# One root product for both pairs of K in an octonion feed-forward kernel, and three reorderings beside it

## What is computed

```
y   = einsum('bct,bcd->bdt', x, W[condition])         # one 64x64 matrix for each of 32 samples
Wq  = scale * clip(round(W / scale), -1, 1)           # scale = mean |W|: ternary weights
M   = einsum('jik,jod->koid', S_OCT, Wq)              # S_OCT: signs of the octonion product
gate, up = einsum('...id,koid->...ko', y, M_gate), ... M_up     # 8 blocks of 128 -> 8 blocks of 342 (341 used)
h   = silu(gate) * up
out = x + einsum('...id,koid->...ko', h, M_down)
```

## Time and profile before

| | |
|---|---|
| median of 3 runs | 679.83 us (679.83 to 680.08) |
| the profiled execution's own time | 679.09 us |
| its span, first to last instruction | 677.3 us |
| PE busy | 643.8 us (95%), 7010 matmuls |
| DVE busy | 516.5 us (76%) |
| POOL busy | 385.1 us (57%) |
| ACT busy | 323.2 us (48%) |
| mean granted TensorE clock | 0.986 |

### The profile page before, as it was taken

One profiled execution on the slowest core, in us unless ns is written; L12 is line 12 of the kernel. 1 busy time (PEld: TensorE's weight loads), 2 busy tenths in 40 slices (PEclk: granted clock), 3 DMA queues, 4 the chain that ended last, 5 costly groups with the idle time before them and its releaser, 6 DMA issues. The chain is left out here.

```text
span 677.3 us, 17118 instructions
## 1 busy us (share of the span) xinstructions
PE 643.8 (95%) x7010; PEld 595.5 (88%) x7010; DVE 516.5 (76%) x873; ACT 323.2 (48%) x542; POOL 385.1 (57%) x453
## 2 busy tenths in 40 slices
PE   3599899999999999999999999999999999999997
PEld 3378699899999999998998999999999999988986
DVE  1899977868776787868877698767878687787785
ACT  4847455345534545254454446254462545434440
POOL 1256685547637576348646476376754486465553
PEclk9799899999999999999999999999999999999997
DMA  9200030140003200041001300031000300021001
GB/s 345 67 2 1 1 116 15 39 155 1 2 2 102 90 2 2 1 137 55 2 2 61 132 1 2 1 126 68 1 2 6 121 1 2 2 72 55 2 1 63
DMA packets 10576, 31.50 MB, mean 47 GB/s; under 512 B 3330, under 2 KB 3330, under 8 KB 10370
## 3 DMA queue, kind: packets, MB, share of 16 engines
q1 hardware_dynamic: 9906, 28.81, 12.3%
q10 hardware_dynamic: 592, 1.61, 0.7%
HBM read 22.02 MB, written 8.39 MB: 45 GB/s over the span
## 5 line engine op out<-in xcount | busy, mean ns | idle before, releaser
L1240 PE MATMUL ps<-y_op,gate_table 128*128 128x256 f16 x1408 | 182.6, 275 | 8.2 <-DVE y_op L979 4.2
L1240 PE MATMUL ps<-y_op,up_table 128*128 128x256 f16 x1408 | 180.3, 273 | 0.2 <-ACT up_table L724 0.2
L1240 PEld LDWEIGHTS ps<-y_op,gate_table 128*128 128x128 f16 x1408 | 138.3, 99 | 27.3 <-issue 4.4
L1240 PEld LDWEIGHTS ps<-y_op,up_table 128*128 128x128 f16 x1408 | 137.9, 98 | 16.8 <-DVE up_table L895 0.7
L617 POOL TENSOR_TENSOR h_pairs<-h_f 128x256 f32<-128x256 f32 (+2 forms) x128 | 118.0, 949 | 60.0 <-ACT h_f L767 57.7
L524 POOL TENSOR_TENSOR o_sb<-o_sb,wd_sb 128x256 f32<-128x256 f32 (+1 forms) x150 | 87.4, 617 | 90.8 <-DVE wd_sb L1108 89.6
L617 POOL TENSOR_TENSOR z_f<-h_pairs 128x512 f32<-128x512 f32 (+1 forms) x80 | 103.7, 1317 | 43.0 <-DVE z_op L995 41.2
L1248 PE MATMUL ps<-third_table,y_op 128*128 128x170 f16 x1408 | 108.2, 237 | 0.6 <-ACT third_table L724 0.6
L1248 PEld LDWEIGHTS ps<-third_table,y_op 128*128 128x128 f16 x1408 | 105.1, 97 | 1.1 <-issue 0.8
L822 ACT ACTIVATE ps<-ps,small 128x512 f32<-128x512 f32 x64 | 42.4, 662 | 111.0 <-DVE ps L1009 85.0
L1401 PE MATMUL ps<-down_u,z_op 128*128 128x256 f16 (+1 forms) x768 | 92.8, 277 | 2.0 <-DVE z_op L995 2.0
(11 more groups left out here) (98 smaller groups left out, 643.2 us busy)
## 6 DMA issues: line engine op xcount, KB each, us to landing
x_in<-in_x_dram SPq DMA_DIRECT2D x8, 1024.0 KB, 5.1
o_sb<-in_x_dram SPq DMA_DIRECT2D x16, 512.0 KB, 3.7
out_dram<-o_sb SPq DMA_DIRECT2D x15, 512.0 KB, 2.7
h_op<-in_L_ffn_w_gate_dram ACTq DMA_DIRECT2D x3, 512.0 KB, 6.8
h_op<-in_L_ffn_w_up_dram SPq DMA_DIRECT2D x3, 512.0 KB, 7.4
z_op<-in_L_ffn_w_down_dram SPq DMA_DIRECT2D x1, 1536.0 KB, 11.4
out_dram<-o_sb SPq DMA_DIRECT2D x2, 256.0 KB, 2.2
cond_bd<-in_L_cond_weights_dram SPq DMA_DIRECT2D x30, 16.0 KB, 3.0
```

What stands on the lines that cost most here:

```text
L1240: mm = pe.matmul(dst, table[m][:, slot, q, :], y_op[:, op, e, :], start=(i == 0 and e == 0), stop=(i == len(terms) - 1 and e == 1))
```

## The change

- **Root product.** Both `shared_pair` products of a window hold the product of weight block `root` (slot 18) once plainly and once negated. The change makes the root product once (`root_pair`, with a new operand 14 of `y_op`, the sum of operands 12 and 13). ACT copies it to `root_sb`. The first pair's own single term is added onto it in the bank. For the second pair ACT writes the negated copy back into the bank (`seed_second_pair`) and PE adds that pair's own term. The root of the next window is made in chunk 3 of the window before it.
- **y and tables.** POOL makes operand 14. The third piece of `y` becomes 7 operands wide (it was 6). Two table slots are now sums that DVE builds, and ACT copies one slot fewer. The power-of-two scale of y is halved.
- **Third window's ternary forms.** POOL makes them, in three passes for gate and three for up, in place of two passes for each on DVE.
- **Boundary.** `y_lo` of the first two pieces stands ahead of the last two `z_lo`. POOL's last round of z begins with the half whose chunks are copied first. PE's first chunk of a tile waits for all of y and starts with the root.
- **Beginning.** The first weight sum on PE comes after one round of y (it was two). DVE sums up's second and third window (it was the third alone). `copy_slots(1, 0)` stands ahead of the sum over the down weights, and `h_scales(0)` stands after `y_lo`.

The core of the diff:

```diff
-    TOP_Y = float(2 ** 14)
+    TOP_Y = float(2 ** 13)
...
-    TERN_AFTER = {1: (1, 1), 4: (0, 2), 6: (1, 2)}
-    TABLE_AFTER = {0: (0, 1), 2: (1, 1), 5: (0, 2), 6: (1, 2)}
+    TERN_AFTER = {1: (1, 1)}
+    TABLE_AFTER = {0: (0, 1), 2: (1, 1), 4: (0, 2), 6: (1, 2)}
     DOWN_AFTER = {0: 0, 3: 1, 5: 2}
...
+    Y_PIECES = [slice(0, 4), slice(4, 8), slice(8, 15)]
...
+    root = wq[0, 0]
+    (jx, one), (jy, other) = root[0], wq[0, 1][0]
+    assert one == other == 1 and wq[1, 0] == wq[0, 1] and wq[1, 1] == weight((jx, -1))
+    ROOT_OP = 14
+    q_own = [(weight((jy, 1), (jx, -1)), 13), (weight((jy, 1), (jx, 1)), 12)]
...
-    NBUILD, NCOPY = 4, 4
+    NBUILD, NCOPY = 6, 3
...
+                pool.wait_ge(y_summed, 6 * T + 5)
+                signed_add(y_f[:, ROOT_OP], y_f[:, 12], y_f[:, 13], 1).then_inc(y_summed, 1)
...
+            def ternary_of_third(m):
+                raw_at, dst = [ap[m][THIRD][:, :, 0:LAST] for ap in (raw, tern)]
+                above = pairs_of_down[:, 0:2].rearrange("p n j o -> p (n j) o")[:, :, 0:LAST]
+                pool.wait_ge(scale_ready, 3 * (m + 1))
+                if m > 0:
+                    pool.wait_ge(third_tern_ready, m)
+                pool.tensor_scalar(above, raw_at, half[m], None, ALU.is_gt).then_inc(third_compared, 1)
+                pool.tensor_scalar(dst, raw_at, minus_half[m], None, ALU.is_lt).then_inc(third_compared, 1)
+                pool.wait_ge(third_compared, 2 * m + 2)
+                pool.tensor_tensor(dst, above, dst, ALU.subtract).then_inc(third_tern_ready, 1)
...
+                if k == NR - 2:
+                    pool.wait_ge(h_copied, NC * T + NC - 2)
                     pool.wait_ge(z_ready, n)
-                pair_up(signed_add, k, h_pairs).then_inc(pairs_ready, 1)
+                    pair_up(signed_add, k, h_pairs, (0,))
+                    pool.wait_ge(h_copied, NC * T + NC)
+                    pair_up(signed_add, k, h_pairs, (1,)).then_inc(pairs_ready, 1)
...
+                    pool.wait_ge(slots_built[1], NBUILD)
+                    ternary_of_third(0)
+                    ternary_of_third(1)
...
+            def copy_root(T, w):
+                act.wait_ge(root_done, root_of(T, w))
+                if w == THIRD:
+                    act.activation(root3_sb, bank_q3, ACT.Copy).then_inc(root_copied, 1)
+                else:
+                    act.activation(root_sb[:], bank_q, ACT.Copy).then_inc(root_copied, 1)
+            def seed_second_pair(T, w):
+                act.wait_ge(root_copied, root_of(T, w))
+                act.wait_ge(q_copied, NU * T + 2 * w + 1)
+                if w == THIRD:
+                    act.activation(bank_q3, root3_sb, ACT.Copy, scale=-1.0).then_inc(q_seeded, 1)
+                else:
+                    act.activation(bank_q, root_sb[:], ACT.Copy, scale=-1.0).then_inc(q_seeded, 1)
...
+                if c == 0:
+                    copy_root(T, 0)
...
+                if c == C3:
+                    seed_second_pair(T, THIRD)
+                if T > 0 and c % 4 == 3 and c < C3:
+                    copy_root(T, c // 4 + 1)
...
+                if c % 4 == 0 and c < C3:
+                    seed_second_pair(T, c // 4)
                 if T == 0:
+                    if c % 4 == 3 and c < C3:
+                        copy_root(T, c // 4 + 1)
...
-            for w in range(NQ - 1):
-                sum_abs_of(1, w)
+            sum_abs_of(1, 0)
             y_hi(0)
+            copy_slots(1, 0)
             act.wait_ge(down_loaded, 16)
-            sum_abs(2 * NQ - 1, raw_down_at, NQ * raw_n, abs_sum[2])
-            copy_slots(1, 0)
+            sum_abs(NQ + 1, raw_down_at, NQ * raw_n, abs_sum[2])
...
+                signed_add(slots_at(m, w, 19, 1), t[:, 7:8], t[:, 4:5], 1).then_inc(built, 1)
+                signed_add(slots_at(m, w, 20, 1), t[:, 7:8], t[:, 4:5], -1).then_inc(built, 1)
...
+            for w in range(1, NQ):
+                dve.wait_ge(up_loaded[w], 16)
+                dve.tensor_reduce(abs_sum[1][:, w:w + 1], raw[1][w].rearrange("p j o -> p (j o)"), AX.X, ALU.add,
+                                  apply_absolute_value=True).then_inc(abs_summed_dve, 1)
             y_scales(0)
-            dve.wait_ge(up_loaded[NQ - 1], 16)
-            dve.tensor_reduce(abs_sum[1][:, NQ - 1:NQ], raw[1][NQ - 1].rearrange("p j o -> p (j o)"), AX.X, ALU.add,
-                              apply_absolute_value=True).then_inc(abs_summed_dve, 1)
             scales(1)
             scales_of_ffn()
-            h_scales(0)
             y_lo(0, range(2))
             ternary_of(1, 0)
             build_table(1, 0)
             y_lo(0, range(2, NY))
+            h_scales(0)
...
+                if T + 1 < NT:
+                    y_lo(T + 1, range(2))
                 for i, k in enumerate(last_rounds(T)):
                     z_lo(T, k, NR - 2 + i)
                 if T + 1 < NT:
-                    y_lo(T + 1)
+                    y_lo(T + 1, range(2, NY))
...
+            def root_pair(T, w):
+                if w == 0:
+                    if T > 0:
+                        pe.wait_ge(q_copied, NU * T)
+                        pe.wait_ge(ud_ready, SUB * (T - 1) + 1)
+                else:
+                    pe.wait_ge(q_copied, NU * T + 2 * w)
+                if w == THIRD:
+                    if T == 0:
+                        for m in range(2):
+                            pe.wait_ge(slots_built[m], NBUILD * NQ)
+                            pe.wait_ge(slots_copied[m], NCOPY * NQ)
+                    for s in range(SUB):
+                        mm = group3(bank_q3[:, s], s, [(slots[root], ROOT_OP)], s == 0)
+                else:
+                    if T == 0 and w > 0:
+                        for m in range(2):
+                            pe.wait_ge(slots_built[m], NBUILD * (w + 1))
+                            pe.wait_ge(slots_copied[m], NCOPY * (w + 1))
+                    for m in range(2):
+                        mm = group(bank_q[:, m], m, [(slots[root], w, ROOT_OP)], m == 0)
+                mm.then_inc(root_done, 1)
+            def wait_for_root(T, w, K):
+                if K == 0:
+                    pe.wait_ge(root_copied, root_of(T, w))
+                else:
+                    pe.wait_ge(q_seeded, root_of(T, w))
...
-                u = NU * T + c // 2
-                if u > 0:
-                    pe.wait_ge(q_copied, u)
-                if T > 0 and c == 0:
-                    pe.wait_ge(ud_ready, SUB * (T - 1) + 1)
+                wait_for_root(T, q, K)
                 for m in range(2):
-                    mm = group(bank_q[:, m], m, [(slots[wq[K // 2, b]], q, 12 + b) for b in range(2)])
+                    mm = group(bank_q[:, m], m, [(slots[q_own[K // 2][0]], q, q_own[K // 2][1])], False)
...
-                    pe.wait_ge(y_ready, NY * T + 2)
-                    own(T, c)
-                    pe.wait_ge(y_ready, NY * T + 3)
-                    shared_pair(T, c)
-                    shared(T, c)
+                    if T > 0:
+                        pe.wait_ge(y_ready, NY * T + 3)
+                        root_pair(T, 0)
+                        own(T, c)
+                        shared_pair(T, c)
...
+                if T > 0 and c % 4 == 3:
+                    root_pair(T, c // 4 + 1)
                 if T == 0:
                     first_tile_at(c, 0)
                 own(T, c)
                 if T == 0:
+                    if c % 4 == 3:
+                        root_pair(T, c // 4 + 1)
...
-            for r in range(2):
-                y_round(0, r)
+            y_round(0, 0)
             sum_abs(0)
-            for r in range(2, 4):
+            for r in range(1, 4):
```

77 lines of the change are left out of this document (52 added, 25 removed).

## The result

The changed kernel takes 673.62 us (median of 4 runs, 672.59 to 674.52), the kernel before 679.83 us (4 runs, 677.98 to 680.08). The ratio is 0.9918, with a 95% interval of 0.990 to 0.9936: faster by 0.8%. I had forecast 666 with a range of 662.5 to 671, so the direction is right and the size is wrong: 6.2 us came where I expected 14.

A forecast was written before the change was run, and what follows sets the result against it. PE was taken to bound seven of eight tiles. Savings of 8.2 (steady tiles), 1.2 (first tile), 1.1 (earlier z) and 3.6 (clock) sum to 14.1 us, giving 665.7 for the median, stated as 666, range 662.5 to 671.

The forecast's parts named there:

- The steady root product: Seven steady tiles: fewer PE matmuls save 8 x 0.109 + 4 x 0.074 = 1.17 us a tile, 8.2 us in all.
- No wait of PE on the root or on the seed: Steady tiles: ACT's root copy and negated seed fit behind other work, the seed with 3 us of slack.
- since PE did not wait there, gives nothing: Boundary between tiles: the new order of y and z costs nothing and gains nothing.
- the 1.2 us of gain: First tile: net gain for the tile, with bounds of 3 us lost and 3.5 us won.
- A gain in front is lost there unless DVE is faster too: First tile, chunk 2's own product: 0 to 2 us of earlier start disappears, as that product waits for DVE.
- the rival that had POOL's forms cost the first tile: First tile: POOL stretches DVE's early work 5 to 7 us, 3 us lost; 670, or 673.5; chance 0.14.
- z comes about 2.1 us earlier, PE starts 1.1 us earlier: Last tile's end: POOL's split round brings z forward; PE's wait falls from 2.0 to about 0.85 us.
- The clock: Last tile's end: with PE's stop under 1 us the clock stays at full pace behind it.
- Together 3.6 us: Last tile's end: full clock shortens 32 matmuls from 6.17 to 3.49 us and the next 96 from 6.19 to 5.2.
- the clock falls again: Rival, last tile's end: the root pays in full but the clock still drops, giving 669.6 us; chance 0.22.

The follow-up runs named there:

- kernel 11: The kernel before with POOL's last pairing of h split in two, no root product: 675.96 us, ratio 0.9950.
- kernel 6: The changed kernel with all of `y_lo` behind the last z again, POOL's split kept: 673.37 us, ratio 0.9915 to the kernel before.
- kernel 2: The changed kernel with POOL's last pairing of h in one piece again: 678.22 us, ratio 0.9986 to the kernel before.
- kernel 1: The changed kernel with only the root product kept; beginning, boundary order, POOL's last round and ternary forms as before: 682.13 us, ratio 1.0038 to the kernel before.
- kernel 3: The changed kernel with the third window's ternary forms on DVE again and its gate table back behind chunk 5: 676.56 us, ratio 0.9958 to the kernel before.
- kernel 5: The changed kernel with the old beginning (weight sum after two rounds of y, `h_scales` ahead of `y_lo`): 673.81 us, ratio 0.9924 to the kernel before.
- kernel 10: The kernel before with only the third window's two ternary forms moved to POOL: 679.14 us, ratio 1.0002.
- kernel 7: The changed kernel with another PE order in the first tile, ready work ahead of root and pair products: 672.14 us, ratio 0.9896 to the kernel before.
- kernel 9: The changed kernel with PE's other first-tile order and 48 correction matmuls ahead of the last wait for z: 668.69 us, ratio 0.9843 to the kernel before.
- kernel 4: The changed kernel with the end filled: 48 correction matmuls moved ahead of the last tile's wait for z; 671.73 us, ratio 0.9891 to the kernel before.
- kernel 8: The kernel before with half of the second subtile's corrections moved ahead of the last wait for z: 678.22 us, ratio 0.9981.
- kernel 12: The kernel before with POOL's ternary forms and POOL's split pairing, without the root product: 677.30 us, ratio 0.9966.

## Why the prediction was wrong, point by point

**The steady root product: right in size, by a sum of three.** In the first two windows PE keeps the 8 x 0.109 us. From a tile's first own product to the third window's main group it takes 42.21 us before. Counting the saving and the 4 root matmuls now made ahead of that group, 41.64 is due, and the trace shows 41.64. In the third window 0.49 us goes back, 0.44 of it in one stretch: from the transpose behind the window's first group to the down start PE took 5.31 us before and 5.75 after. 0.28 of it is booked as the wait on `pu_sb`: the window is shorter, and DVE's work on the last chunk before it is not. From first own product to down start the root thus saves 0.68 and not 1.17 us. The last tile, which makes no y for a next one, doesn't give it back: there PE takes 5.30 us over the same stretch before and after, and from kernel 11 to the changed one its step shrinks by the full 1.17 (74.40 to 73.23). The rest of the step's 1.03 comes from the boundary (0.35), which kernel 11 shows to be POOL's split. So the root gave 5.25 us of the 8.2 (543.54 - 538.29), and the split made up for most of the rest by luck. "No wait of PE on the root or on the seed" was right for these tiles: ACT had the room.

**The boundary: "since PE did not wait there, gives nothing" is a step that failed.** PE did wait, by 0.35 us a tile. In the earlier trace rows the wait is booked as 0.19 us of issue and the row before it ends by a modelled time, so I read none. The starts of the two rows show it: 3.85 us for 32 matmuls that take 3.49 elsewhere. With the root alone the same place names its releaser, DVE's `o_sb`, which frees the first bank. Counted from the down start it begins at 19.2 us in kernel 11 and at 21.0 before. My order of credit was wrong as well. The early `y_lo`, which I had filling DVE's gap, is worth nothing with the split (kernel 6) and costs 0.35 us a tile without it (2 against 1).

**The first tile: the 1.2 us of gain failed by 1.7 in the profiled pair, by 1.2 if A is called level.** "A gain in front is lost there unless DVE is faster too" looked right, as chunk 2 came at the same instant as before. Kernels 3 and 5 say otherwise. With the old beginning chunk 2 would be 1.7 us later (44.40), so the gain in front did reach it. What took it there is the extra work between: POOL's six passes, which took 14.2 us against my 11, account for about 1.2 us of it (kernel 3 against after). But the passes don't cost the tile: with the root's six-sum tables, and with the third gate table moved forward beside them, they save 2.9 us by the medians. In the kernel before, without that move, they save nothing (kernel 10). So the rival that had POOL's forms cost the first tile is refuted on its sum, though its sign was seen (a stop over 3 us, the lower clock behind it). What did cost is what I left without a price: PE's waits on the root (1.2 and 1.04 us) and on the third table (1.85), of which another order of PE gives 1.5 back (kernel 7). The Trainium skill (GPSIMD Engine Reference, opening) speaks against elementwise work on GpSimd. The trace agrees that POOL is slower (three passes for each form, 14.2 us, against two on DVE, 3.7), and the measurement disagrees on the verdict in this one tile, where PE waits for DVE's turn.

**The end: "z comes about 2.1 us earlier, PE starts 1.1 us earlier" failed.** POOL's half of z came 1.4 us earlier. PE's start moved 0.3 us the other way, as the last tile's third window is shorter too and the down start comes earlier against DVE: with the root and no split (kernel 2) PE starts 15.8 us after the down start, 0.4 later than before. DVE makes the other half of that z itself. Beside POOL's earlier z, DVE's last round takes 3.31 us for 2.23. Every last tile with the split shows it, and those without (before, kernels 1, 2, 9 and 10) have 2.23. So the chain that ends last now goes through DVE and ACT. I had followed the releaser named in the rows of before and not asked who is late next. In kernel 11, where the split is alone, PE starts on z 0.13 us earlier than before, and with the root it is 0.13 too (kernel 2 against after): this is what the move was worth. The stop stayed at 2.3 us.

**The clock.** My step was that the clock stays up behind a short stop, read from one stop of 1.3 us that kept it and two of 2.0 and 4.2 us that lost it. The filling points to the stop as a condition: in kernels 4, 8 and 9 PE doesn't stop and the products on z run at 2.4 GHz. Of the eleven profiled executions with a stop nine fell. But its length doesn't decide. After 2.27 us the changed kernel fell to 1.2 GHz, after 2.28 kernel 5 didn't; after 1.83 us kernel 12 fell and kernel 11 didn't. What decides between them stays open.

**"Together 3.6 us": the price of the clock was wrong too.** I counted PE's rows alone. In the five profiled executions that kept the clock behind z (kernels 4, 5, 8, 9, 11) it is 14.7 to 14.8 us from PE's first product on z to the end of the span, against 15.8 before. So keeping the clock was worth 1.0 us over the kernel before and not 3.6, since ACT, DVE and the output transfer then end last, 5.7 to 8.4 us after PE. Losing it as the changed kernel did cost 2.2 us more than before lost. At least 2.6 us of the forecast were not there to be won.

**The sum by the runs.** Steady tiles: 7.6 us in place of 8.2, of which the split is 2.4 (545.91 - 543.54). First tile: 0.5 lost in the profiled pair in place of 1.2 won. End: 2.5 lost in place of 4.7 won, which is 1.4 us at PE's start on z and 5.8 at the clock. 9.5 us are missing in the profiled pair, 7.2 of them at the end. The filling gave 3.0 of those back. By the medians 7.9 are missing. The likeliest rival was "the clock falls again", at 669.6; it happened, and three things lay on top: the first tile, DVE's last round, and a half clock longer than before's.

## What to carry to other kernels

When one of two engines that make halves of the same buffer is moved earlier, cost the other half beside it before you count the gain: here both touch SBUF, and the second half took over the path. A row whose idle time reads "issue", right behind one whose end is modelled, may hide a real wait; compare steps of whole tiles instead. Where PE stops briefly before its last work, put independent matmuls in front of the wait: that gave 1.9 us here (0.9 in the kernel before), where the earlier producer moved PE's start by 0.13. And price a faster PE at the end by the chain behind it: once PE is done early, copies, sums and the transfer set the end.

## What the runs showed of the hardware

- DVE and POOL stretch each other on the same SBUF work. POOL's z took 2.82 us with DVE nearly idle (before, steady tiles) and 4.34 beside `y_lo` (kernel 2); six table sums took 1.12 us alone and 4.75 beside POOL. How much falls on which engine isn't fixed: DVE's two last sums of 85x512 took 3.31 us beside POOL's z of 3.27 in the last tile, and 2.25 beside a z of 3.88 in the steady tiles of the same kernel, where `y_lo` follows. Why, no run tells.
- POOL's single-input comparison of 680 elements took 3.98 us the first time, beside DVE's `y_lo`, and 2.27 the second; the sum of two f16 operands of the same size 1.48 both times.
- The granted clock of TensorE, 2.4 or 1.2 GHz, took opposite turns behind stops of the same length to 0.01 us, in the same place of the same work (kernels 11 and 12).
